# Decayed scores of a retention layer: one written-out pipeline over 32 tiles with a third turned buffer, and two unused products in front of each score

## The reference

```python
x_norm = rmsnorm(x, ln_w)
latent = silu(x_norm @ Wc)
q, k, v = split(latent @ Wqkv, 3)               # heads of 32
q_f, k_f = elu(rope(rmsnorm(q))) + 1, elu(rope(rmsnorm(k))) + 1
kv_input = einsum('blhd,blhe->blhde', k_f, v_f) * gate * dt
z_input = k_f * dt
kv_states = cumsum(kv_input / safe_z, axis=1) * df      # df = decay ** position
z_states = cumsum(z_input / safe_z, axis=1) * df
out_num = einsum('blhd,blhde->blhe', q_f, kv_states)
den = clip(sum(q_f * z_states), 1e-5)
out = rmsnorm(out_num / den, mem_w)
h = h + (out @ Wp) * silu(latent @ Wg)
```

## Time and profile before

| | us |
|---|---|
| median of 3 runs | 2861.12 |
| lowest, highest | 2820.07, 2864.53 |
| the profiled execution | 2859.32 |
| its span (first to last instruction) | 2857.5 |
| TensorE, VectorE, ScalarE, GpSimd busy | 2308.8, 2043.2, 1794.6, 1556.8 |
| the decayed scores | 431.49 to 658.04 |

### The profile page before, as it was taken

One profiled execution on the slowest core, in us unless ns is written; L12 is line 12 of the kernel. 1 busy time (PEld: TensorE's weight loads), 2 busy tenths in 40 slices (PEclk: granted clock), 3 DMA queues, 4 the chain that ended last, 5 costly groups with the idle time before them and its releaser, 6 DMA issues. The chain is left out here.

```text
span 2857.5 us, 49077 instructions
## 1 busy us (share of the span) xinstructions
PE 2308.8 (81%) x12375; PEld 1616.9 (57%) x12376; DVE 2043.2 (72%) x3473; ACT 1794.6 (63%) x5092; POOL 1556.8 (54%) x1661
## 2 busy tenths in 40 slices
PE   4519006776756999999999999999999999857783
PEld 2305005555654666666666666666666666657673
DVE  6811563336017999999999999999999999674554
ACT  2203213221544888888888888888888888605652
POOL 2240560001643776777777777677776777615552
PEclk8755556555886999999999999999999999958987
DMA  6310000003120000000000000000000000041114
GB/s 207 103 33 0 0 0 1 0 0 96 44 60 1 0 0 1 0 0 0 0 0 0 0 0 0 0 0 0 0 0 0 0 0 0 5 106 37 40 38 108
DMA packets 67637, 63.03 MB, mean 22 GB/s; under 512 B 20864, under 2 KB 54656, under 8 KB 67584
## 3 DMA queue, kind: packets, MB, share of 16 engines
q1 hardware_dynamic: 49008, 40.88, 5.1%
q0 software_dynamic: 8192, 16.87, 2.3%
q10 hardware_dynamic: 10384, 4.66, 0.6%
HBM read 48.71 MB, written 13.68 MB: 22 GB/s over the span
## 5 line engine op out<-in xcount | busy, mean ns | idle before, releaser
L1754 POOL TENSOR_TENSOR attend_weights<-attend_weights,attend_scales 128x512 f32<-128x512 f32 x1024 | 1047.1, 1044 | 470.2 <-DVE attend_scales L1670 470.2
L1648 DVE TENSOR_REDUCE attend_maxima<-attend_psL 128x16 fp32r<-128x1024 f32 x512 | 624.2, 1219 | 79.4 <-PE attend_psL L1570 79.4
L1664 DVE TENSOR_REDUCE attend_sums<-attend_weights 128x16 f32<-128x1024 f32 x512 | 618.6, 1208 | 0.1
L1714 ACT ACTIVATE attend_turned<-attend_psT 128x512 f32<-128x512 f32 x1024 | 555.5, 599 | 4.2 <-PE attend_psT L1589 3.8
L1589 PE MATMUL attend_psT<-consts,attend_weights 128*128 128x128 f32 x4096 | 530.5, 272 | 0.8 <-POOL attend_weights L1754 0.8
L1589 PEld LDWEIGHTS attend_psT<-consts,attend_weights 128*128 128x128 f32 x4096 | 477.1, 140 | 69.9 <-POOL attend_weights L1754 2.9
L1602 PE MATMUL attend_psA<-attend_turned,attend_chunk_values 128*64 128x512 f32 x2048 | 495.9, 605 | 0.8 <-ACT attend_turned L1714 0.8
L1708 ACT ACTIVATE attend_weights<-attend_psL,attend_maxima 128x64 f32<-128x64 f32 x2048 | 446.6, 329 | 54.0 <-DVE attend_maxima L1648 54.0
L1569 PE MATMUL attend_psL<-keys,attend_q_high 128*128 (+1 forms) x1024 | 434.5, 424 | 1.6 <-ACT attend_q_high L1693 1.6
L1570 PE MATMUL attend_psL<-keys,attend_q_low 128*128 (+1 forms) x1024 | 404.4, 395 | 0.0
L1700 ACT ACTIVATE attend_weights<-attend_psL 128x512 f32<-128x512 f32 x512 | 314.1, 613 | 0.0
(11 more groups left out here) (317 smaller groups left out, 3004.9 us busy)
## 6 DMA issues: line engine op xcount, KB each, us to landing
select_xbuf<-in_x_dram SPq DMA_DIRECT2D x16, 1024.0 KB
select_emb<-L_attn_video_embeds_dram ACTq DMA_DIRECT2D x16, 256.0 KB
moe2back_back<-result SPq DMA_DIRECT2D x8, 512.0 KB, 7.2
normed<-moe2route_normed SPq DMA_DIRECT2D x4, 520.0 KB, 8.8
moe_w<-in_L_ffn_W_dram SPq DMA_DIRECT2D x1, 2048.0 KB, 10.8
normed<-moe1route_normed SPq DMA_DIRECT2D x4, 512.0 KB, 5.1
moe1back_back<-result SPq DMA_DIRECT2D x4, 512.0 KB, 6.7
moe_w<-in_L_ffn_w_dram SPq DMA_DIRECT2D x1, 2048.0 KB, 11.8
```

The lines of the kernel that those rows point to most:

```text
L1648: dve.tensor_reduce(maxima[:, both, :].rearrange("p j v -> p (j v)"), psL[:, both, :].rearrange("p j (v f) -> p (j v) f", f=FR), X, ALU.ma ...
L1664: dve.tensor_reduce(sums[:, both, :].rearrange("p j v -> p (j v)"), weights[:, both, :].rearrange("p j (v f) -> p (j v) f", f=FR), X, ALU. ...
L1714: act.activation(turned[:, parity, :, j * P:(j + 1) * P], psT[:, j % 2, :].rearrange("p (k q) -> p k q", k=SUB), ACT.Copy).then_inc(turned ...
L1754: pool.tensor_tensor(w, w, scales[:, s, :, None].to_broadcast([P, VC, FR]), ALU.mult).then_inc(normalised, 1)
```

## The change

The loop `turns` becomes `in_turn`: one pipeline of 37 steps, written out for all 32 tiles, with fixed addresses. So `stage_tile` and its buffer fall away, and `turn_tile` reads `qkv` itself. `qkT` and `qdiag` have three buffers (`TURNED`), and `spread` waits for the heads of tile g-3. TensorE turns a tile ahead of the score of the tile before it, and VectorE keeps the state ahead of the mask. In front of each score stand two products of the fp32r identity and the first 512 columns of the keys into the same `psS`; the score, which starts its sum afresh, overwrites them. The tile `params` of the projection is now freed before this block.

```diff
-            stage = sb2("stage", [P, 2, 2 * D])
-            qkT = sb2("qkT", [P, 2, 2 * P])
-            qdiag = sb2("qdiag", [P, 2, H0, P])
+            TURNED = 3
+            qkT = sb2("qkT", [P, TURNED, 2 * P])
+            qdiag = sb2("qdiag", [P, TURNED, H0, P])
...
-                with engine.Fori(0, B // 2) as it:
-                    for k in range(PT + STAGES - 1):
-                        for stage_of, lag in stages:
-                            if 0 <= k - lag < PT:
-                                n = k - lag
-                                stage_of(it * PT + n, n, (it * 2 + n // TB) * (TB - 1) + n % TB)
...
+                for k in range(G + STAGES - 1):
+                    for stage_of, lag in stages:
+                        if 0 <= k - lag < G:
+                            g = k - lag
+                            stage_of(g, g // TB * (TB - 1) + g % TB)
...
-                        act.wait_ge(acc_ready, g + 1)
-                        act.activation(qkT[:, n % 2, :], psQK[:, n % 2, 0:2 * P], ACT.Copy)
+                        if g >= TURNED:
+                            act.wait_ge(acc_ready, g + 3 - TURNED)
+                        act.activation(qkT[:, g % TURNED, :], psQK[:, g % 2, 0:2 * P], ACT.Copy)
...
-                    turns(act, (stage_tile, 0), (spread, 1), (copy_o, 4))
+                    in_turn((spread, 1), (copy_o, 4))
...
-                    turns(dve, (mask, 2), (keep_state, 1), (finish, 5), (divide, 3))
+                    in_turn((keep_state, 1), (mask, 2), (finish, 5), (divide, 3))
...
+                        for _ in range(2):
+                            pe.matmul(psS[:, g % 2].rearrange("p h l -> p (h l)"), K.ident_r[:], K.keys[:, 0:H0 * P], start=True, stop=True)
...
-                    turns(pe, (score, 2), (turn_tile, 1), (project, 5), (turn_o, 4), (add_up, 3))
+                    in_turn((turn_tile, 1), (score, 2), (project, 5), (turn_o, 4), (add_up, 3))
```

More of the change, by code:

```diff
@@ L471, in retention @@
             latT = sb1("latT", [LAT, 2, L])
+            params = sb1("params", [P, G, H0, 4])
             sg = params
@@ L776, in retention, with in_turn @@
                 "acc_ready", "acc_used", "o_ready", "o_root_ready", "o_steps", "oT_ready", "oT_copied", "y_ready", "y_read", "y_added"))
-            PT = 2 * TB
             STAGES = 6
-            def turns(engine, *stages):
-                with engine.Fori(0, B // 2) as it:
-                    for k in range(PT + STAGES - 1):
-                        for stage_of, lag in stages:
-                            if 0 <= k - lag < PT:
-                                n = k - lag
-                                stage_of(it * PT + n, n, (it * 2 + n // TB) * (TB - 1) + n % TB)
+            def in_turn(*stages):
+                for k in range(G + STAGES - 1):
[3 more added lines that the diff above has]
+                            stage_of(g, g // TB * (TB - 1) + g % TB)
             with nc.Block() as block:
@@ L840, in _, with mask, keep_state, divide @@
                     dve.nop().then_inc(y_added, 2)
-                    def mask(g, n, m):
+                    def mask(g, m):
                         dve.wait_ge(acc_ready, g + 1)
                         dve.wait_ge(scores_ready, g + 1)
-                        dve.tensor_tensor(probs[:, n % 2], psS[:, n % 2], K.const("causal")[:, None, :].to_broadcast([P, H0, P]),
+                        dve.tensor_tensor(probs[:, g % 2], psS[:, g % 2], K.const("causal")[:, None, :].to_broadcast([P, H0, P]),
                                           ALU.mult).then_inc(probs_ready, 1)
-                    def keep_state(g, n, m):
-                        if n % TB == TB - 1:
+                    def keep_state(g, m):
+                        if g % TB == TB - 1:
                             return
                         dve.wait_ge(state_ready, m + 1)
-                        dve.tensor_tensor(state[:, n % 4, :], psW[:, 0:H0 * V1], K.const("headblock"), ALU.mult).then_inc(state_masked, 1)
-                    def divide(g, n, m):
+                        dve.tensor_tensor(state[:, g % 4, :], psW[:, 0:H0 * V1], K.const("headblock"), ALU.mult).then_inc(state_masked, 1)
+                    def divide(g, m):
                         dve.wait_ge(acc_ready, g + 3)
@@ L862, in divide @@
                         acc = psA[:, 0:H0 * V1].rearrange("p (h e) -> p h e", h=H0)
-                        out = o[:, n % 2, :]
+                        out = o[:, g % 2, :]
                         dve.tensor_scalar(den[:, 0, :], acc[:, :, DH0], 1e-5, None, ALU.max).then_inc(o_steps, 1)
@@ L870, in divide, with finish @@
                         dve.wait_ge(acc_used, g + 2)
[L871 removed]
+                        dve.tensor_tensor_reduce(osq[:], out, out, 1.0, 0.0, ALU.mult, ALU.add, oms[:, g % 2, 0:1]).then_inc(o_steps, 1)
                         dve.wait_ge(o_steps, g * 3 + 3)
[L873 to L875 removed]
+                        dve.tensor_scalar(oms[:, g % 2, 1:2], oms[:, g % 2, 0:1], 1.0 / D, RMS_EPS, ALU.mult, ALU.add).then_inc(o_ready, 1)
+                    def finish(g, m):
                         dve.wait_ge(o_root_ready, g + 1)
@@ L895, in values_of, with turn_tile @@
                     def values_of(g):
[L896 to L901, removed]
+                        return qkv[:, g, 2 * D:]
+                    def turn_tile(g, m):
+                        if g % TB < TB - 1:
                             pe.wait_ge(state_masked, m + 1)
-                            pe.matmul(psW[:, 0:H0 * V1], stage[:, n % 2, D:2 * D], values_of(g), start=(n % TB == 0), stop=True,
+                            pe.matmul(psW[:, 0:H0 * V1], qkv[:, g, D:2 * D], values_of(g), start=(g % TB == 0), stop=True,
@@ L905, in turn_tile @@
                                       skip_group_check=True).then_inc(state_ready, 1)
                         pe.wait_ge(qdiag_set, g + 1)
-                        pe.transpose(psQK[:, n % 2, 0:P], stage[:, n % 2, 0:D], ident)
-                        pe.transpose(psQK[:, n % 2, P:2 * P], stage[:, n % 2, D:2 * D], ident).then_inc(qkT_ready, 1)
-                    def score(g, n, m):
+                        pe.transpose(psQK[:, g % 2, 0:P], qkv[:, g, 0:D], ident)
+                        pe.transpose(psQK[:, g % 2, P:2 * P], qkv[:, g, D:2 * D], ident).then_inc(qkT_ready, 1)
@@ L912, in score @@
+                    def score(g, m):
                         pe.wait_ge(qdiag_set, g + 3)
                         pe.wait_ge(probs_ready, g + 1)
-                        pe.matmul(psS[:, n % 2].rearrange("p h l -> p (h l)"), qkT[:, n % 2, P:2 * P], qdiag[:, n % 2].rearrange("p h l -> p (h l)"),
+                        for _ in range(2):
+                            pe.matmul(psS[:, g % 2].rearrange("p h l -> p (h l)"), K.ident_r[:], K.keys[:, 0:H0 * P], start=True, stop=True)
+                        pe.matmul(psS[:, g % 2].rearrange("p h l -> p (h l)"), qkT[:, g % TURNED, P:2 * P], qdiag[:, g % TURNED].rearrange("p h l -> p (h l)"),
@@ L916, in score, with add_up @@
                                   start=True, stop=True).then_inc(scores_ready, 1)
-                    def add_up(g, n, m):
+                    def add_up(g, m):
                         pe.wait_ge(acc_used, g + 1)
-                        first = n % TB == 0
+                        first = g % TB == 0
                         if not first:
                             pe.wait_ge(state_masked, m + 1)
-                            pe.matmul(psA[:, 0:H0 * V1], qkT[:, n % 2, 0:P], state[:, (n - 1) % 4, :], start=True, stop=False, skip_group_check=True)
+                            pe.matmul(psA[:, 0:H0 * V1], qkT[:, g % TURNED, 0:P], state[:, (g - 1) % 4, :], start=True, stop=False, skip_group_check=True)
```

36 lines of the change are left out of this document (16 added, 20 removed).

## The result

The changed kernel takes 2704.42 us in the median of four runs (2704.11 to 2743.0), the kernel before 2859.61 us beside them (2820.07 to 2864.53). The ratio is 0.9535, with a 95% interval of 0.9394 to 0.9675. Like with like, 2704 stands against 2820, and 2743 against 2860: the change is worth about 116 us, a ratio of 0.959 in either group. The 0.9535 mixes the groups: three of four runs were in the faster one after, and one of four before.

What follows compares the result with a forecast made beforehand. TensorE at the low clock plus a 1.52 us wait per tile bound the decayed stage. Steps of 21.5 and 95 us plus 9 us make 126 against 226.5; 100.5 less than 2859.3 gives 2758 us, range 2715 to 2803.

Steps and rivals of the forecast that it cites:

- if it lies elsewhere, 2719 is possible: Lowest earlier run, 2820.1 us, is 39 us under the profiled one; if that luck lies outside the decayed stage, 2719.
- The ring: Decayed scores: heads, copy and spread, next score wait in turn; a third buffer removes TensorE's 1.52 us wait, 48 us.
- D: Rival, chance 0.03: spread still ends after TensorE is ready for the score; 1.52 us hole and low clock stay; 2893 us.
- The drains: Decayed stage: the pipeline emptied after each of four loop turns; removing three is worth only some 5 us.
- the straight-line code: Written-out decayed stage: price of instruction fetching, between 0 and 20 us, taken as 0.
- The products: Two unused products before each score: 0.92 us a tile at low clock, 0.46 high; wide work that helps the clock rise.
- The clock: Largest term: TensorE in the decayed stage, without holes, rises to 2.4 GHz by the fourth step and holds.
- A: Main case, chance 0.79: the clock rises and stays in the decayed stage; 2758 us.
- B: Rival, chance 0.12: the decayed stage's clock goes up and down; 2789 us at half each, 2803 at a third high.
- the first turn's 0.63: Granted clock of the old loop's first 8 tiles, taken to suggest a third of the time high: 45 us more, 2803.
- The high-clock step: One decayed tile at 2.4 GHz, summed from TensorE's start-to-start times: 3.4 us, for steps 5 to 32, 95 us.
- The tail: From the last score to the decayed stage's end: 12.1 us at the low clock, 9 us after the change.

## Why the prediction was right, and where it was not

*The size.* I forecast 2758 us with a range of 2715 to 2803, and faster by over 2%. The direction and the main mechanism were right; the median came out 11 us below the low end. Two things add up. The stage took 107.4 us where I had 126, 19 us less. And the profiled execution that I subtracted from had a low projection, while three of the four runs after had a high one, 39 us less. Which group a run falls into is luck: the fourth run, 2743.0 us, lies within the range. The prediction named that case ("if it lies elsewhere, 2719 is possible"), but its number took none of the 39 us off. They lie elsewhere, in the projection; the luck within the stage is some 9 us.

*The ring.* Right. Copy and spread run beside the score, and the hole is gone. D, that it stays, did not come.

*The drains, and the straight-line code.* No cost of fetching shows in the stage, 0 as taken. The value of writing out was underrated only in company: some 5 us by my sum; 7 to 16 us alone (217 or 227 to 210), no more than the stage's own spread allows to say; and 45 us once turning stands ahead (180 to 135), where the mean clock is 0.96 in place of 0.70. That the missing drains are what lets it hold is not shown.

*The products.* Their duration was right: 0.46 us a pair was taken, and 0.49 measured for the second pair; the first costs 0.46 in a step without waits, and 0.38 in the mean. Their role was wrong. The step of the prediction that failed is the sentence that the stretch "from turning through products and score to the state" makes the rise: without the products it rises in the same step. What the runs show in its place: from 0.57 in the written-out pipeline with two buffers and the old order, the third buffer alone lifts the clock to 0.93, and turning ahead alone to 0.96. The first closes most of the hole, the second shortens it and moves it; whether its length or its place counts there stays open. The products cost 12 us and give nothing in this kernel. In the kernel before they lift the clock to 0.72, and the stage's 215.8 us are within 2 us of the 217.3 that it took without them.

*The clock.* A was right: it rose and stayed. It rose at about 400.5, within the third step, where I had four steps at the low clock: 9 us of the difference. B did not come. Its price was also read too low: the first turn's 0.63 is a quarter of the time at the high clock, not a third, and by the prediction's own steps that is 5.3 us a step and about 2810, beyond the range.

The section "A second HAM failure mode: psum-queue depth-cycling" of the Trainium skill's page "TensorE: Matmul & The Clock Gate" reports frequent small idle times of TensorE between groups of products and a clock that flips. The changed kernel is no test of it, since TensorE has no idle time there (40.00 of 40 us). The kernel before plus products agrees, with a clock that flips at a mean of 0.72. The pipeline with two buffers and no products does not: a hole of 1.0 us in every 4.0 us, and a mean of 0.96.

*The high-clock step.* 3.4 us was too long: the 29 steps from the score at 402.57 to that at 491.71 take 3.07 us in the mean. The sum of rows gave each tile a state product and a state term, which a sequence's last and first tile lack (those steps are 2.7 us). And some terms were too long, taken from rows next to a wait: output turning and state term 0.41 us, where in the stream they are 0.34, the heads 0.93 for 0.81, the score 0.96 for 0.86; the state product was too short, 0.23 for 0.30. That is 9 us over 28 steps. VectorE was just covered, as taken: 2.67 us busy of 3.22.

*The tail.* 8.4 us from the last score to the end, against 9.

## What to carry to other kernels

A recurring hole costs more than its length where it decides which of its two levels the clock takes: close the hole first, by order and buffers, and look at the clock again before paying for unused products. Measure such an edit together with the others too, since the same rewriting was worth 7 to 16 us with one order of TensorE and 45 with the other. Before a gain of a few us is believed, the same stage of the unchanged kernel has to be read from more than one profile. Where a stage has two durations from run to run, look at the microseconds just ahead of it; a few products there can settle it.

## What the runs showed of the hardware

I had not expected that the projection, in which TensorE has no hole at all for 80 us, could stay at 1.2 GHz for its whole length, and in other runs at 2.4 GHz for all but its first 5 us. Its query products have 64 rows of contraction. What it keeps seems to be settled at its start: no trace has the clock rise after 206.5 us or fall before the end, and 14 products of 128 rows by 512 columns ahead of it gave the high level in 16 of 16 runs. Whether the 64 rows are the reason was not tried.

Recurring holes can go with either level: 1.0 us in a 4.0 us step held 2.4 GHz, while 1.5 us in a 7.1 us step stayed at 1.2, at a larger busy share (5.57 of 7.08 us against 97.98 of 134.59). With the products in the kernel before, even 1.5 us in steps of 4.4 us went at 2.4 GHz for two holes in a row. So the busy share of the trace does not foretell the level by itself; which property does, these runs leave open.
